# The first norm of a batch made one iteration earlier, in the value stage of a cross-attention and routed FFN kernel

## What is computed

```python
x = x + attention(layernorm(x), ctx, ctx, Wq, Wk, Wv, Wo)   # 64-token blocks in a band pattern,
                                                            # softmax inside each block pair, sums over pairs
n = layernorm(x)
e = argmax(softmax(n @ gate_w.T))                           # one of two routed experts for each token
routed = relu(mask_e * n @ w1[e] + b1[e]) @ w2[e] + b2[e]   # summed over both experts
shared = relu(n @ sw1 + sb1) @ sw2 + sb2
x = x + routed + shared
```

## Time and profile before

| | |
|---|---|
| median of 3 runs | 1034.85 us (1033.58 to 1035.83) |
| the profiled execution's own time | 1025.89 us |
| its span in the trace | 1024.1 us |
| PE busy | 876.7 us, 86% of the span |
| DVE busy | 536.4 us, 52% |
| POOL busy | 491.5 us, 48% |
| ACT busy | 450.5 us, 44% |
| the loop's twelve iterations (223.6 to 898.3 us) | 674.7 us, 56.2 us each |

### The profile page before, as it was taken

The page is one execution under the profiler, slowest core; times in us unless marked ns, Lnnn a source line. Parts: engine busy times, 40 slices in busy tenths (PEclk is TensorE's granted clock), DMA queues, the critical chain, the costliest instruction groups (busy, mean ns, idle before and its releaser), DMA issues.

```text
span 1024.1 us, 22039 instructions
## 1 busy us (share of the span) xinstructions
PE 876.7 (86%) x7751; PEld 732.4 (72%) x7751; DVE 536.4 (52%) x1090; ACT 450.5 (44%) x991; POOL 491.5 (48%) x798
## 2 busy tenths in 40 slices
PE   3377788998989898998989898989999898978897
PEld 2154666685859687786868696877868686957897
DVE  6556456383727465573837373655638372715200
ACT  3151443444454544444444545444444445442553
POOL 6442524254454636364544546363645545452553
PEclk8576797999999999999999999999999999989999
DMA  8866572909375583919193755839191937444600
GB/s 236 194 200 159 166 177 62 262 27 283 58 254 94 182 166 102 243 55 263 42 280 62 251 98 184 165 99 249 52 264 41 279 61 262 67 168 160 250 11 11
DMA packets 90481, 159.69 MB, mean 156 GB/s; under 512 B 8448, under 2 KB 80512, under 8 KB 85840
## 3 DMA queue, kind: packets, MB, share of 16 engines
q1 hardware_dynamic: 76432, 77.92, 35.0%
q10 hardware_dynamic: 4032, 58.72, 14.6%
q0 software_dynamic: 9984, 22.61, 7.8%
HBM read 119.84 MB, written 39.38 MB: 155 GB/s over the span
## 4 chain that ended last, share of the span: by engine, by line
PE 36%; DMA 16%; issue 16%; POOL 14%; DVE 6%; ACT 2%; SPq 1%; ACTq 1%; POOLq 1%; DVEq 0%
DMA rowin<-queue 9%; PE hid L467 9%; PE acc L675 9%; POOL hl L1337 7%; PE num L540 4%; PE den L547 3%; PE work L522 3%; PE work L587 2%; DMA QP<-scratch_m 2%; DMA queue<-rows,pos 2%; POOL rstd L1329 2%; PE work L573 2%; ACT PT L841 2%; POOL x1b L1344 2%; DMA scratch_m<-mT 1%
## 5 line engine op out<-in xcount | busy, mean ns | idle before, releaser
L1337 POOL TENSOR_TENSOR hl<-h,hh 128x256 fp32r<-128x256 f32 x272 | 203.4, 764 | 223.8 <-ACT hh L862 223.7
L1026 DVE TENSOR_REDUCE nmax<-work 128x8 f32<-128x512 f32 x256 | 163.0, 682 | 25.5 <-PE work L507 25.1
L841 ACT ACTIVATE PT<-work 128x512 f32<-128x512 f32 x256 | 134.0, 604 | 90.6 <-PE work L522 90.3
L1032 DVE COPY T<-num 128x512 f32<-128x512 f32 x64 | 44.2, 691 | 221.7 <-PE num L540 221.7
L522 PE MATMUL work<-QP,KP 128*128 128x256 f32 x512 | 97.0, 312 | 56.5 <-ACT PT L841 34.8
L522 PEld LDWEIGHTS work<-QP,KP 128*128 128x128 f32 x512 | 71.9, 195 | 89.9 <-ACT PT L841 48.4
L862 ACT ACTIVATE h<-hid,bias 128x256 f32<-128x256 f32 x160 | 76.9, 481 | 115.6 <-PE hid L467 114.6
L507 PE MATMUL work<-KP,QP 96*128 96x512 f32 x256 | 99.1, 465 | 30.1 <-DMA QP<-scratch_q 18.5
L467 PE MATMUL hid<-XS,WS 128*128 128x256 f32 x768 | 109.3, 293 | 3.6 <-DVE idle L1194 3.6
L467 PEld LDWEIGHTS hid<-XS,WS 128*128 128x128 f32 x768 | 101.8, 199 | 5.8 <-DVE idle L1194 4.5
L467 PE MATMUL hid<-XR,WR 128*128 128x256 f32 x672 | 90.7, 284 | 0.8 <-issue 0.8
(11 more groups left out here) (238 smaller groups left out, 1665.5 us busy)
## 6 DMA issues: line engine op xcount, KB each, us to landing
WR<-wx ACTq DMA_DIRECT2D x28, 2048.0 KB, 11.2
KP<-scratch_k SPq DMA_DIRECT2D x96, 128.0 KB, 7.6
QP<-scratch_q SPq DMA_DIRECT2D x96, 128.0 KB, 9.1
scratch_k<-T SPq DMA_DIRECT2D x16, 512.0 KB, 3.3
scratch_q<-T SPq DMA_DIRECT2D x16, 512.0 KB, 2.9
wx<-WR POOLq DMA_DIRECT2D x16, 512.0 KB, 4.3
stages<-wraw POOLq DMA_DIRECT2D x24, 256.0 KB, 4.7
xin<-x SPq DMA_DIRECT2D x16, 256.0 KB, 10.2
```

The lines of the kernel that those rows point to most:

```text
L841: nc.scalar.activation(PT[:, j % 8].rearrange("p t q -> p (t q)"), work[:, BANK[("st", j)], :], ACT.Exp).then_inc(sem["exp_done"], 1)
L1026: nc.vector.tensor_reduce(nmax[:, t, 8 * p:8 * p + 8], work[:, BANK[("s", j)], :].rearrange("q (b k) -> q b k", k=BLOCK), AX_X, ALU.max, n ...
L1032: nc.vector.tensor_copy(T[:, 2 * v:2 * v + 2, :], num[:, :, :]).then_inc(sem["num_copied"], 1)
L1337: nc.gpsimd.tensor_tensor(R(hl[:, k % 2, a]), h32[:, k % 2, a], hh[:, k % 2, a], ALU.subtract).then_inc(sem["hl_done"], 1)
```

## The change

The norm of batch `n` moves from iteration `n - 1` to iteration `n - 2`. The statistics stand on DVE behind the next batch's query split, ahead of the value stage. The reciprocal deviation stands on POOL between `add_routed` and `select_bias`. The apply stands on DVE behind the third numerator copy. `xin` is loaded one batch further ahead, at the same place of SP's stream. The norm of batch 1 is made ahead of iteration 0, and that of batch 2 in iteration 0, for which SP loads `xin` right behind iteration 0's bounces. On POOL the low part of unit 6 now stands ahead of `token_ids`. The loop is one iteration shorter, and iteration 14 is written out without the norm. The whole diff, without its unchanged surroundings where these say nothing:

```diff
@@ -368,10 +368,12 @@
                 sp.dma_start(w.rearrange("p m q c -> p (m q c)"),
                              wx[P * e:P * e + P, k].rearrange("p m q c -> p (m q c)")).then_inc(sem[done], 16)
 
-            def iteration(i, more, loads=True):
+            def iteration(i, more, loads=2):
                 shift(i)
                 if more:
                     bounces(i + 1)
+                if type(i) is int and i == 0:
+                    load_x(2)
                 if type(i) is not int or i >= 2:
                     load_tile(i)
                 if type(i) is not int or i >= 1:
@@ -379,9 +381,10 @@
                 if more:
                     sp.wait_ge(sem["st_full"], HEADS * (i + 1))
                     spread(16 * (i + 1), "q_bounced", "k_bounced")
-                if more and loads:
+                if more and loads > 0:
                     load_ctx(i + 2)
-                    load_x(i + 2)
+                if more and loads > 1:
+                    load_x(i + 3)
                 if type(i) is not int or i >= 1:
                     store(i)
 
@@ -412,15 +415,16 @@
             sp.wait_ge(sem["kp_zeroed"], 1)
             sp.wait_ge(sem["qp_zeroed"], 1)
             spread(16, "first_q_bounced", "first_k_bounced")
+            load_x(1)
             sp.wait_ge(sem["consts_made"], 1)
             load_residual(0, first=True)
             load_ctx(1)
-            load_x(1)
             for i in range(LAG):
                 iteration(i, True)
-            with sp.Fori(LAG, LAST - 1) as i:
+            with sp.Fori(LAG, LAST - 2) as i:
                 iteration(i, True)
-            iteration(LAST - 1, True, loads=False)
+            iteration(LAST - 2, True, loads=1)
+            iteration(LAST - 1, True, loads=0)
             iteration(LAST, False)
 
             sp.wait_ge(sem["sel_done"], LAST)
@@ -1152,7 +1156,7 @@
                     if by_vector(n):
                         split_low(n)
 
-            def iteration(i, more):
+            def iteration(i, more, ahead=True):
                 later = present(("x2T", 0), i)
                 maximum(i, 0)
                 maximum(i, 1)
@@ -1175,14 +1179,8 @@
                     gate_scores(i - 1, 1)
                     choose(i - 1)
                 slot(i, 3)
-                for j in range(11, 14):
+                for j in range(11, 16):
                     maximum(i, j)
-                if more:
-                    norm1_stats(i + 1)
-                maximum(i, 14)
-                maximum(i, 15)
-                if more:
-                    norm1_apply(i + 1)
                 low(i, "mT_hi", work[:, BANK[("mT", 0)], 0:P], mT[:, 0, :], mT[:, 1, :], "m_lo")
                 if active(i, 0):
                     finish_routed(i)
@@ -1197,11 +1195,15 @@
                 slot(i, 5)
                 if more:
                     front_qk(i + 1)
+                if ahead:
+                    norm1_stats(i + 2)
                 dve.wait_ge(sem["q_bounced"], 16 * (i + more))
                 dve.wait_ge(sem["k_bounced"], 16 * (i + more))
                 for v in range(VISITS):
                     slot(i, 6 + v)
                     numerators(i, v)
+                    if v == 2 and ahead:
+                        norm1_apply(i + 2)
                 invert(i)
                 if present(("rT", 0), i):
                     routed_low(i - 2)
@@ -1245,15 +1247,18 @@
             dve.wait_ge(sem["bias_summed"], 1)
             nc.vector.tensor_tensor(bias2[:, :], bias2[:, :], flat(mT), ALU.add) \
                 .then_inc(sem["consts_made"], 1)
+            norm1_stats(1)
             dve.wait_ge(sem["consts_made"], 1)
             for n in range(EARLY_PIECES):
                 if by_vector(n):
                     split_low(n)
+            norm1_apply(1)
             for i in range(LAG):
                 iteration(i, True)
-            with dve.Fori(LAG, LAST) as i:
+            with dve.Fori(LAG, LAST - 1) as i:
                 iteration(i, True)
-            iteration(LAST, False)
+            iteration(LAST - 1, True, ahead=False)
+            iteration(LAST, False, ahead=False)
 
             halves = "p (c t) -> p c t"
 
@@ -1516,7 +1521,6 @@
                 slot(i, 3)
                 hidden_low(i, 4)
                 if more:
-                    reciprocal_deviation(i + 1, 0)
                     context_low(i + 1)
                 slot(i, 4)
                 hidden_low(i, 5)
@@ -1531,12 +1535,15 @@
                     add_routed(i)
                 for w in range(6, 9):
                     slot(i, w)
+                if ahead:
+                    reciprocal_deviation(i + 2, 0)
                 if type(i) is not int or i >= 2:
                     select_bias(i)
+                hidden_low(i, 6)
+                if type(i) is not int or i >= 2:
                     token_ids(i)
                 slot(i, 9)
-                for k in (6, 7):
-                    hidden_low(i, k)
+                hidden_low(i, 7)
                 hidden_low(i + 1, 0)
 
             nc.gpsimd.memset(power[:, :], -0.5).then_inc(sem["zeroed"], 1)
@@ -1564,6 +1571,7 @@
             for n in range(EARLY_PIECES):
                 if not by_vector(n):
                     split_low(n)
+            reciprocal_deviation(1, 0)
 
             pool.wait_ge(sem["k_spread"], 96)
             pool.wait_ge(sem["q_spread"], 96)
@@ -1571,9 +1579,10 @@
                 load(n)
             for i in range(LAG):
                 iteration(i, True)
-            with pool.Fori(LAG, LAST) as i:
+            with pool.Fori(LAG, LAST - 1) as i:
                 iteration(i, True)
-            iteration(LAST, False)
+            iteration(LAST - 1, True, ahead=False)
+            iteration(LAST, False, ahead=False)
 
 
             pool.wait_ge(sem["row_loaded"], 16 * (LAST - 1))
```

## The result

| | before | after |
|---|---|---|
| median of 4 runs each | 1034.98 us (1033.58 to 1035.83) | 1021.62 us (1015.95 to 1023.01) |
| the profiled execution's own time | 1025.89 us | 1023.01 us |
| its span | 1024.1 us | 1021.2 us |
| the loop's twelve iterations | 674.7 us | 665.7 us |
| from the span's start to iteration 3 | 223.6 us | 230.5 us |

The ratio of the times is 0.9875 [0.9851, 0.99]: 13 us faster, where 19 were predicted. The profiled execution of the kernel before was one of its fastest: its later runs beside the experiments lie between 1025 and 1038 us. The two traces alone would therefore show too small a difference.

The account below looks back on a forecast made before the run. PE, busy 86% of the span, bounds the kernel, so gains come from its gaps: loop -16.6, start +2, -3 and -1.5 make -19.1 us, from 1034.85 to 1016 us; own range 1011 to 1021, wider range 1007 to 1027.

Parts of the forecast that it names:

- three signs of being wrong: Tile/spread waits grow as much as turn shrinks; tile issued later than 14.7 us behind transpose; iteration 0's maxima much after 37.
- The turn: Between iterations, from last maxima to transposed scores: waits removed gain 0.77 + 0.61 = 1.38 us an iteration.
- it goes whole: PE's wait for the maxima before its transpose vanishes entirely: 0.77 us an iteration.
- `ones_n` comes well ahead of the key projection: With the apply gone from the turn, PE's 0.34 us wait goes; with `xhat`'s 0.27 that gains 0.61 us.
- a new wait of about 0.6 us for `T` takes the place of most of the 0.85 us for the shift: At the third transposed score, PE waits for the query split's low part, so the 1.2 us sooner shift gains little.
- the far end: Turn gain of 0.77 + 1.2 = 1.97 us an iteration, if the sooner shift counts in full.
- I count no loss: At the tile and spread behind the turn, their waits were expected to take nothing from its gain.
- The clock: Rival: TensorE clock falls, 1.45 us each, in all twelve iterations cost 9 us more, 1025 us; chance 0.12 on the bad side.
- +2, -3 and -1.5: Time changes in us for the start with iteration 0, for iteration 1's `idle` wait, and for iteration 2's loop-like waits.
- the upper value: Apply taking 1.70 us as in the turn, instead of 0.81, costing up to 0.4 us an iteration, 5 us in all.
- the weights overtake the append: Rival: append packets queue behind the weights, delaying SP's tile load to about 528.3; slower, 1050 us; chance 0.05.
- The tile holds the gain: Rival: tile's transfer keeps its time behind the transpose, loop gains only 12 x 0.77 = 9 us; 1023 us; chance 0.16.

Follow-up runs that it names:

- The full stall: Changed kernel with two useless DVE statistics after ACT's rounding, ahead of the maxima's low part, in iterations 3 to 15: 1021.76 us, ratio 0.9905 to the kernel before.
- the halved kernels: Kernel before and changed kernel, each loading half the expert weights' bytes in the loop: 1007.46 us before, 998.54 us after.
- the second trace: Changed kernel, unchanged, timed and profiled again beside the experiments: 1020.48 us, ratio 0.9867 to the kernel before.
- The two traces of the kernel before: Kernel before, unchanged: first profiled execution 1025.89 us, profiled once more 1035.49 us.
- the old start: Changed kernel with the norms of batches 1 and 2 and the early loads back in their old places: 1015.4 us, again 1014.6 us.
- the run with the later weights: Changed kernel with ACT's issue of the expert weights behind the sixth exponential instead of the fourth: 1031.71 us, ratio 1.0 to the kernel before.
- sooner weights: ACT's weights issue behind the second exponential instead of the fourth: 1016.65 us on the kernel before, 995.12 us on the changed kernel with old first norms.
- The fastest version: Changed kernel with batches 1 and 2's norms in old places and weights issued behind the second exponential: 995.12 us, ratio 0.9646 to the kernel before.
- early residual load: Changed kernel with batches 1 and 2's norms in old places, residual's load moved on SP ahead of the shift: 1011.11 us, ratio 0.9797 to the kernel before.

## Why the prediction was right, and where it was wrong

The direction and the range were right: 1021.6 us lies in 1007 to 1027, just past the slow end of the forecast's own range of 1011 to 1021. But of the three signs of being wrong that the prediction names, one came true in full, as the tile is issued at 19.7 us behind the transpose and not at 14.7. The waits for the tile and the spread grew by 13.9 us in the loop, more than half of what the turn shrank by (12 x 1.97 = 23.6), and iteration 0's maxima start at 38.6 us, 1.6 past the third sign's 37. That the time came out near the forecast is therefore in part luck. Three of its steps have to be told apart.

*The turn* was the mechanism, and it was undersized. The steps "it goes whole" and "`ones_n` comes well ahead of the key projection" hold, and the low part's start was estimated at 0.7 us and measured at 0.66. The step "a new wait of about 0.6 us for `T` takes the place of most of the 0.85 us for the shift" failed: with a shift that starts 1.2 us sooner the first transposed scores start 1.2 us sooner too, and the third waits about 0.1 us. The term behind it was "the 0.61 us that PE gains on its way to the projection": the key projection starts 3.03 - 1.94 = 1.09 us sooner behind the transpose, and the query split ends 7.81 us behind it where it was 8.85. I had read iteration 1's wait as a rule. The turn gains 0.77 + 1.2 = 1.97 us, the far end, and without long transfers behind it 2.1.

*"I count no loss"* behind the turn was the second failure, and it ate what the first had left out. The waits for the tile and the spread took much of it back, 13.9 us more within the loop. The full stall shows the outcome: the shift's 1.2 us are worth 0.1 to 0.3 us an iteration. What survives should then be mostly the wait for the maxima, which comes behind the tile and the spread and is hidden by neither; no run isolates it.

The clock's part is not the one that the halved kernels show. In the kernel before, the six iterations with a fall, always in the value stage, take 56.3 us on the mean and the six without one 56.1: where the clock has fallen PE never waits for the tile, and where it has not it waits 0.3 to 1.6 us, so such a fall costs next to nothing. The rival's price of 1.45 us for each was too high. In the changed kernel's first trace the seven iterations without a fall take 54.8 us on the mean, 1.4 less than before. But in three the clock falls elsewhere, 28 to 42 us behind the transpose, just behind the wait for the tile or the spread, and these take 56.2 to 58.1 us; the second trace has three such iterations too, at 57.1 to 57.6. The two traces of the kernel before have none in the loop. Iteration 5 (windows view, and PE's timeline ahead of the fall):

```profile
341.88:399.97 58.09, 51.52 (x477) 44.08 (x475) 30.34 (x65) 26.19 (x58) 28.16 (x48) 0.97 0.62 154
383.70:387.10 3.40, 3.40 (x17) 3.21 (x16) 2.35 (x5) 1.57 (x4) 0.97 (x2) 0.50 0.00 0
...
382.30 0.73 PE L511 MATMUL work<-KP,QP 96*128 96x512 f32 x2 [2.55 <-DMA QP<-scratch_q]
```

Over the 54.8 us these three iterations lose 7.4 us, in longer waits and in slower matmuls; which brings the other is not shown.

From the first score to the maxima transpose the loop took 17.0 us before and takes 16.1 after. The traces of the loop give 9 to 14 us for twelve iterations, the medians with the old start 17 to 18.5, and the sum had 16.6. That the sum's loop term (16.6 us) is near the medians, and near the 1.4 us of the iterations without a fall, is two errors that cancel; the difference between traces and medians is within what executions of one kernel differ by.

*The start* is the term that made the forecast too fast: "+2, -3 and -1.5" are 2.5 us gained, and the traces lose 6.9 and 6.3 (5 to 7 by the medians). The "+2" measured 5.9 and 5.2, the "-3" of iteration 1 -1.2 and -0.8, and the "-1.5" of iteration 2 +2.2 and +2.0: there the tile, which lands with the weights, is waited for 5.02 us, and 4.3 in the second trace. Here the rows showed what a norm costs where DVE is idle, but not that it isn't idle in iteration 0. Batch 2's `xin` held DVE for 9.49 us, POOL's reciprocal stood behind splits, and the division waited for both. POOL's loads moved by 4.2 us instead of 2.5. The wait for `idle` gave 2.2 of the 3 us. The loop's tile wait was read off the row of the weight load (5.5 us, 7 times); PE's own is 4.1 us, 6 times, which changes nothing in the sum.

The apply's price was right: 0.81 us were taken, 0.73 measured. The Trainium skill's rule for the upper value, a shared port pair of VectorE and GpSimd (*SBUF — State Buffer*, section "SBUF: two separate sides"), agrees with 1.70 us in the turn. In the loop's new place no operation of POOL stands beside the apply; in iteration 1 two splits of POOL do, and there it takes 1.37 us.

Of the rivals, *the weights overtake the append* was judged by its price when it should have been judged by its mechanism. It happened: SP sat at the tile's load for 5 us longer. The DMA view of the changed kernel shows the queue q0, which the append shares with the scatter of the results, and the weights in q10, first 520.9 to 525.0 us and then 524 to 526 us:

```profile
q10 hardware_dynamic: 76, 1.25, 97.4%
...
q10 hardware_dynamic: 45, 0.74, 88.5%
q0 software_dynamic: 19, 0.08, 9.5%
```

From 520.9 to 525.0 us q0 has no packet at all, while 76 of q10 go. In iteration 8 of the kernel before q0 is as empty for 4.2 us, but the packets of both appends have gone before that begins. The step of the rival that fails is the next one, a transfer of the load's own behind the weights: the tile lands when the weights do, whenever it was issued. In the run with the later weights it was issued 3.4 us sooner and in iteration 8 landed 0.4 us sooner behind the transpose. The Trainium skill, *DMA: Bandwidth & Descriptors*, section "Queues, rings and completion order", has the engines go round their queues packet by packet. For those 4 us the trace shows no such taking of turns, though the second append had been issued at 519.83; whether q0 had a packet ready then, it does not show. From then on it agrees in kind, for packets of both queues go side by side (19 and 45 above), and the append gets through before all the weights have landed. The measured delay of the load is 5 us. *The tile holds the gain* (1023 us) came nearest to the measured time, and its loop term of 9 us is near the 9 to 14 of the traces; but its 2.5 us gained at the start have the wrong sign, and the tile did not keep its place behind the transpose: its transposes start 26.4 us behind it in iteration 8 (535.44 - 509.01), where it was 27.1 in iteration 9 before. *The clock* did not fall in every iteration; in the first trace it fell six times, in five of the twelve, in the second in ten, in the halved one in eight.

What stays open: why executions of one kernel differ by 1%; why the later weights cost 10 us; on what, beside the gaps, the clock's falls depend; and whether norm and sooner weights add up or do more, for which 21.5 against 18 us is too small a difference. The fastest version together with the early residual load was not tried.

## What to carry to other kernels

A removed wait is worth what no transfer behind it takes back: find the next point at which the engine waits for a long load, and count only what lies behind that point, until a stall put in the same place says otherwise. Look at which issue starts the long load and what stands ahead of it on its engine; moving two lines there brought as much as the whole reordering. When work is moved one iteration sooner for a steady loop, price the first iterations by their own rows, for the slots that are idle in the loop may be full there; the old order can be kept for them.

## What was not expected of the hardware

The tile's load, which waits for the small packets of the append, went 5 us later once the 4 MB of weights were issued 0.12 us behind the second append instead of 1.4 us, and the append's queue stood empty for 4 us meanwhile; with half a microsecond more between them the load was 1.6 us later. With half of that load's bytes the kernel before took 25 us less, and its clock did not fall once in the loop, where it fell six times at full bytes; eleven of its iterations agreed within 0.3 us, where those of the full kernels differ by up to 4. And at half the bytes the shorter iterations came with clock falls: none in the loop before, eight after. A fall in the value stage cost 0.2 us of an iteration in the kernel before, where the wait for the tile comes behind it and takes it up, and 1.6 us at half the bytes, where there is no such wait.
